# Layer-1 weight rows spread over more turns, and the first cross items' projections placed later

## The reference

```python
xn = _adaln(x, noise_emb, ln1_w, ln1_b)               # layer 0: self attention
q, k, v = jnp.split(xn @ qkv_w.T, 3, axis=-1)
sa = _attn(_rope(q), _rope(k), v) @ sa_out_w.T
x = x + sa
xn = _adaln(x, noise_emb, ln2_w, ln2_b)               # layer 1: cross attention
q = _rope(xn @ q_w.T)
k, v = _rope(context @ k_w.T), context @ v_w.T
x = x + _attn(q, k, v) @ ca_out_w.T
xn = _adaln(x, noise_emb, ln3_w, ln3_b)               # feed-forward
x = x + (gelu(xn @ ffn_w1.T + ffn_b1) @ ffn_w2.T + ffn_b2)
```

## Time and profile before

| | us |
|---|---|
| median of three executions | 1949.46 |
| lowest, highest | 1944.86, 1951.01 |
| profiled execution, its own time | 1946.9 |
| span of the profile | 1945.1 |
| TensorE busy | 1878.5 (97%) |
| ScalarE busy | 1388.9 (71%) |
| VectorE busy | 1298.7 (67%) |
| GpSimd busy | 789.8 (41%) |

### The profile page before, as it was taken

How to read it: one execution, slowest core, us unless ns; L and a number is a source line. 1 busy time by engine, 2 the same in 40 slices (tenths; PEclk the granted TensorE clock), 3 DMA queues, 4 the chain that set the end, 5 groups by cost and what they waited for, 6 DMA issues and landing times. The chain is left out here.

```text
span 1945.1 us, 39403 instructions
## 1 busy us (share of the span) xinstructions
PE 1878.5 (97%) x13460; PEld 1639.8 (84%) x13460; DVE 1298.7 (67%) x2248; ACT 1388.9 (71%) x3813; POOL 789.8 (41%) x820
## 2 busy tenths in 40 slices
PE   8799999999998999999999997899999999999999
PEld 6678888888887888888888875688898989999898
DVE  6766677676677677676776665446667676766754
ACT  3577778788877888888888886655656566565654
POOL 4433343343343454454454432013445354454531
PEclk9899999999999999999999998999999999999999
DMA  6766566666668667667667676253231323223130
GB/s 208 217 196 208 169 186 205 177 183 202 183 190 229 202 205 229 200 198 226 198 203 220 200 210 166 77 160 123 73 107 57 109 59 115 77 87 98 55 98 33
DMA packets 307348, 308.38 MB, mean 159 GB/s; under 512 B 21968, under 2 KB 260944, under 8 KB 307152
## 3 DMA queue, kind: packets, MB, share of 16 engines
q1 hardware_dynamic: 304528, 304.47, 51.8%
q10 hardware_dynamic: 2624, 1.39, 0.3%
HBM read 212.46 MB, written 92.27 MB: 157 GB/s over the span
## 5 line engine op out<-in xcount | busy, mean ns | idle before, releaser
L850 DVE TENSOR_REDUCE neg_max<-ps_s 128x2 f32<-128x512 f32 x512 | 350.2, 687 | 227.6 <-PE ps_s L603 227.3
L733 ACT ACTIVATE ps_s<-ps_s,neg_max 128x256 f32<-128x256 f32 x1024 | 455.1, 446 | 46.7 <-DVE neg_max L850 42.7
L747 ACT ACTIVATE prob<-ps_s 128x512 f32<-128x512 f32 x512 | 305.6, 597 | 136.8 <-PE ps_s L622 124.9
L914 POOL TENSOR_TENSOR rope_c<-rope_c,rope_s 128x256 f32<-128x256 f32 x128 | 98.0, 765 | 343.6 <-DVE rope_s L825 343.6
L622 PE MATMUL ps_s<-qT,kT 98*128 98x256 f32 x1024 | 215.5, 292 | 13.1 <-DMA qT<-max_rows 8.1
L603 PE MATMUL ps_s<-kT,qT 96*128 96x256 f32 x1024 | 213.6, 290 | 10.4 <-ACT ps_s L733 8.5
L603 PEld LDWEIGHTS ps_s<-kT,qT 96*128 96x128 f32 x1024 | 171.7, 191 | 55.8 <-ACT ps_s L733 22.7
L593 PE MATMUL ps_g<-xx_hi,w_hi 128*128 128x256 f32 x1024 | 209.8, 286 | 6.5 <-DVE rope_s L825 5.1
L733 ACT ACTIVATION_READ_ACCUMULATOR ps_s<-ps_s,neg_max 128x1 f32 x1024 | 209.9, 205 | 0.0
L593 PE MATMUL ps_g<-xx_lo,w_hi 128*128 128x256 f32 x1024 | 206.8, 284 | 0.0
L593 PE MATMUL ps_g<-xx_hi,w_lo 128*128 128x256 f32 x1024 | 206.7, 283 | 0.0
(11 more groups left out here) (154 smaller groups left out, 4666.6 us busy)
## 6 DMA issues: line engine op xcount, KB each, us to landing
kT<-k_turned SPq DMA_DIRECT2D x384, 128.0 KB, 3.0
qT<-q_turned SPq DMA_DIRECT2D x128, 256.0 KB, 3.7
f_raw<-in_w1T SPq DMA_DIRECT2D x124, 256.0 KB, 3.0
k_turned<-rot_hi SPq DMA_DIRECT2D x64, 256.0 KB, 3.2
k_turned<-rot_lo SPq DMA_DIRECT2D x64, 256.0 KB, 2.7
q_turned<-rot_hi SPq DMA_DIRECT2D x64, 256.0 KB, 3.4
q_turned<-rot_lo SPq DMA_DIRECT2D x64, 256.0 KB, 3.5
qT<-q_turned SPq DMA_DIRECT2D x128, 128.0 KB, 3.7
```

The lines of the kernel that those rows point to most:

```text
L733: ins = eng.activation(scores[:, t * L:(t + 1) * L], scores[:, t * L:(t + 1) * L], ACT.Exp, bias=neg_max[G % 2][:, t, j:j + 1], accum_out= ...
L747: eng.activation(prob[:, n % NP, :, :].rearrange("p t l -> p (t l)"), ps_s[:, score_bank(step), :], ACT.Exp).then_inc(exp_done, 1)
L850: eng.tensor_reduce(neg_max[G % 2][:, :, j], ps_s[:, score_bank(step), :].rearrange("p (t l) -> p t l", l=L), AX.X, ALU.max, negate=True). ...
L914: eng.tensor_tensor(rope_c[n % 2][:, 0, :], rope_c[n % 2][:, 0, :], rope_s[:, 0, :], ALU.subtract)
```

## The change

The 12 rows of weights for k, q and v of layer 1 are one list with five places between rows, from p - 4 at i = 14. The steps that prepare items 16, 17, 18 and 19 are put later by 24, 18, 12 and 6 places (for item 16 the load, the split and the projections; its turn_x goes from p + 31 to p + 42, while its stats, norm and scale stay; for items 17 to 19 all steps). Item 16 loses its own places for q, and v of all four is spread over 9 places.

```diff
             late = {N: 26, N + 1: 14}.get(ahead, 0)
+            held = {B: 24, B + 1: 18, B + 2: 12, B + 3: 6}.get(ahead, 0)
+            if ahead > B:
+                late += held
...
-            x_place = p + late + (31 if ahead == B else 18 if B < ahead < N else 16)
+            x_place = p + late + (42 if ahead == B else 18 if B < ahead < N else 16)
...
-                put(p - 10, "ctx_load", ahead)
-                put(p + 9, "ctx_split", ahead)
+                put(p - 10 + held, "ctx_load", ahead)
+                put(p + 9 + held, "ctx_split", ahead)
...
-                turns(spread(p + 18, 11, k))
-                spread(*((p + 42, 9, v) if ahead == B else (p + 42, 13, v)))
+                turns(spread(p + 18 + held, 11, k))
+                spread(p + 42 + held, 9 if held else 13, v)
             if ahead < N - 1:
-                turns(spread(*((p + 42, 13, q) if ahead < B else (p + 50, 10, q) if ahead == B else (p + 29, 13, q))))
+                turns(spread(*((p + 42, 13, q) if ahead < B else (p + 29 + held, 13, q))))
...
         if i == B - 2:
-            weight_rows(p + 6, layer_rows(1, "k"), 3, 8)
-            weight_rows(p + 19, layer_rows(1, "q"), 3, 8)
-            weight_rows(p + 28, layer_rows(1, "v"), 3, 8)
+            weight_rows(p - 4, [row for m in "kqv" for row in layer_rows(1, m)], 5, 8)
```

## The result

The changed kernel took 1963.12 us in the median of five executions (from 1960.56; one took 2085.97 and is left out of the ratio), the kernel before, run beside it, 1949.46. The ratio is 1.0076, with 95% between 1.0058 and 1.0093: slower by 11 to 18 us. A second comparison gave 1.0073 [1.0060, 1.0086]. The forecast was 1952.5, its range 1941 to 1960.

What follows compares the result with a forecast made beforehand. TensorE, busy 97%, bounds the kernel, so time can come only from where it is not fed. Gains 1.1 + 0.6 + 0.8 = 2.5 against costs 4.8 + 0.8 = 5.6: 3.1 us slower, median 1952.5, range 1941 to 1960.

Steps and rivals of the forecast that it cites:

- A: Gap at turns 234 to 238, where TensorE waits for ScalarE and max_rows: cost 8.9 us before, 7.8 forecast, gain 1.1.
- X: End of ScalarE's total(233) in A; total(235) was forecast 5.1 us later, scores(238) 7.9 us later at full clock.
- The credit of 8.9: Cost of A before the change: 5.7 us of TensorE idle and 3.2 of slow matmuls.
- The waits for w_raw go: ScalarE's waits for w_raw vanish with weight rows at fives, turns 222 to 241: cost 0, or 1.0.
- I take half, 0.8: TensorE's early wait of 1.6 us for max_rows, turn 221: half of it gained, bounds 0 and 1.6.
- the 0.6: A single TensorE wait of 0.6 us goes, as its stretch has half the products: gain 0.6.
- SP's queue: ctx_load(17) at p+56 waits for x_low(16) at p+49, so it does not block what is behind it.
- B, C and D: New holes without products at turns 249 to 251, 264 and 265, 278 and 279: 2.3, 0.7, 1.8, together 4.8 us.
- Rival 1: TensorE's lead hides the new gaps and the clock stays up in A: gains of 5.8 us, 1943.7; chance 0.27.
- rival 3: The moves cancel wholly, since TensorE's work is the same: 1949; chance 0.08.
- the slower rival: The clock falls behind B, C and D, first products at 1.2 GHz: 8.8 us slower, 1958.3; chance 0.20.
- T1: Experiments' theory: held projections empty A's turns; filling holes wins 3 to 6, 4 to 7, both 6 to 9 us.

Runs made afterwards that it cites:

- winning edit: The kernel before with only the k products of item 16 moved, to p + 29 over 13 places: 1941.37, 0.9978; again on another chip 1943.44, 0.9974.
- the pads: The changed kernel with matmuls of no use in its emptied turns (234 to 237, 249 to 251, 264, 265, 278, 279): 1960.48, 1.0061.

## Why the prediction was wrong

- *"The gap at 234 to 238, called A ... Gain 1.1".* This step failed, and with it the sign of what comes before B: a gain of 2.5 was summed, a loss of 6.7 came. By the prediction's own reckoning A cost 12.7 us instead of the forecast 7.8: from the scores at 601.82 to those at 618.45 pass 16.6, with 1.92+0.14+1.9 = 3.96 of TensorE's work in them. (The same sum before is 4.68 and not 4.8, so A cost 9.0 there.) The walk from X holds: with X = 605.8, total(234) ended at X+2.2 (608.0) and total(235) at X+5.3 (611.1), where 5.1 was forecast. Three things around it do not. The landing was taken from the one copy of before, 4.6, though the change itself brings the loads that lengthen it; it was 7.8, so scores(238) came at X+12.6 instead of X+7.9, or X+10.4 with the 2.5 that the forecast added for the clock. The time before X was put at 0.7 idle; it was 3.10 at scores(235) alone. And the walk began too late: turns 230 to 233 had lost eight of their sixteen units, so TensorE ran into ScalarE there already (1.51 at 596.79, scores(231)), and turn 226 lost 1.31 where it had lost 0.43. The 1.51 differs between executions: in the second profile of the changed kernel it is 0.21 and item 14 takes 47.1, so the time is lost somewhere in these turns each time, behind different waits.
- *The credit of 8.9.* The 8.9 us of before were read as a gap that other things could mend. The winning edit shows what most of it was: four turns without a product. The change took further products away from it and forecast it shorter.
- *"The waits for w_raw go ... Cost 0, and 1.0 if that cover went".* They did not go: 0.42, 3.52 and 1.70, as loads took 6.5 us and SyncE's queue, which issues them, was held at rot_lo. The spacing of the rows did not make them: with the old rows and the projections held, ScalarE waited 5.9 for w_raw, and 5.6 in the changed kernel. On its own this matters little: with the loads earlier the time moved by 2 us, within the interval.
- *"I take half, 0.8" of the early wait for max_rows, and the 0.6.* The first stayed 1.60 (0.34 in the second profile of the changed kernel), the second became the 1.51 above.
- *"SP's queue ... does not block what is behind it".* The context load did not, but behind A the queue stood 9.3 us for the turn_x of item 16, which the change had put later; what that cost isn't shown.
- *B, C and D, 4.8 and 0.8 for the clock.* The mechanism and place were right: new idle at 651.09 to 654.73, 690.97 to 692.92 and a smaller one at 730.30. Idle in B is 0.65+1.40+0.88 = 2.9 (2.3 forecast), in C 0.90+0.97 = 1.9 (0.7 forecast), in D 0.68 (1.8 forecast): 5.5 against 4.8. The clock fell behind B and C, not D. The losses of items 15 to 17 sum to 9.6 against the 5.6 forecast. The clock's term was too small: half of one fall, 0.8, was taken, and two came, 2.4 by the pads and 3.5 by the table. Rival 1, a lead that hides the holes, and rival 3, a full cancelling, are out.
- *The rule of the Trainium skill, "TensorE: Matmul & The Clock Gate", section on "psum-queue depth-cycling".* It was set as the slower rival, with a fall behind each of B, C and D. This trace agrees with it at two of the three: short idle times of 0.65 to 1.40 us between matmuls and 3.4 us at 1.2 GHz behind B and behind C, but none behind D, where one idle time of 0.68 stood. The rival's price, 8.8 slower, came nearer to the measured 14 than the forecast, but it has the same gain of 2.5 before B in it, where 6.7 were lost.

"The total work of TensorE is thus the same" was right and was the key, not used to its end: if the engine that bounds runs some 35.66 us an item from item 19 on in either kernel, time lost by idling early is given back nowhere in these items. ScalarE is busy 32.06 of 38.00 us beside it, so it has little slack for turns that have lost their products; they pass at ScalarE's pace, with TensorE idle. How much of the loss is idle time and how much the clock is settled behind B and C only, and the prices that T1 put on filling single holes of the changed kernel came out too high.

## What to carry to other kernels

Where the bounding engine is fed from a queue of movable work, count for every stretch how much of that work each version puts there, and lay it into the bare turns before anything else: the k products put eleven places later filled the hole and won 5 us, the same products and all behind them twenty-four later went past it and lost 14. If several waits end within a microsecond or two of each other, take none of them as the cause from its length; here removing one only named the next. A landing time read from the trace belongs to the traffic of that moment, above all to what was issued ahead of it, so read it again from a stretch as full as the change will make it.

## What the runs showed of the hardware

- The weigh behind max_rows (two 8 KB transfers) began 4.6 us after their copy began where the DMA engines had been 0.43 busy ahead of it and were 0.92 busy in between, and 7.8 us with 1.08 and 1.10. Without the res load in front it was 6.5, with 1.07 in between.
- The stretches at the lower clock were 3.4 us long behind B and C (6.8 behind B in some of the runs) and 3.4 to 13.7 around A. Behind B it fell after idle times of 0.65, 1.40 and 0.88 in 4.5 us, behind C after 0.90 and 0.97; behind the single 0.68 at 730.30 it did not.
- The length of one idle time does not settle whether the clock falls. A wait for max_rows near 570 us brought no fall with 1.59 before and 1.60 in the second profile of the winning edit, and a fall with 1.60 in the changed kernel and 1.95 in the winning edit's first profile. One of 1.92 in B brought a fall at 652.7 with v of items 16 to 18 over 12 places, and none when v of item 15 was spread as well.
